# A decoder pipeline that runs on over the rounds, with the copy of the scores moved to the exponentials

## The chip, the cores and the metric

The kernel runs on one core of a Trainium2 chip. The metric is the device time of one execution in microseconds (us). The engines are TensorE (PE; its weight loads are PEld), VectorE (DVE), ScalarE (ACT), GpSimd (POOL) and the DMA queue of SyncE (SP). The profile is of one execution.

## What is computed

Two layers over 64 sequences of 128 tokens with 128 features, in float32: six stages, each written to memory and read by the next (a Mamba block, cross attention, an expert layer, a trajectory layer, a decoder layer, a quantised feed-forward layer). The change is in the fifth, the decoder layer. Cut to what matters:

```python
x_self  = _prob_sparse_self_attn(x, out_w, out_b)     # 16 heads, 128 keys, top-k of each row kept
x = _layernorm(x + x_self, ln1_g, ln1_b)
x_cross = _mha_cross(x, memory, in_w, in_b, out_w, out_b)   # 16 heads, 77 keys, plain softmax
x = _layernorm(x + x_cross, ln2_g, ln2_b)
h = jax.nn.gelu(x @ ffn_w1.T + ffn_b1, approximate=False)
x = _layernorm(x + h @ ffn_w2.T + ffn_b2, ln3_g, ln3_b)
```

The self attention has no projections of its own: queries, keys and values are the token features. The number kept by its top-k is ceil(log(129)) = 5.

## The kernel before

`decoder_stage` goes over the 64 sequences in 16 groups of four (GB = 4). Its rounds are software pipelined by group: in round i the self attention is of group i + 1, the cross attention of group i, and the feed-forward part of group i - 1. So there are 18 rounds, -1 to 16: five written out, and a loop (`nc.Fori`) over rounds 1 to 14, which are the full ones. Every round is a block: at its end all engines meet at a barrier and all semaphores are cleared.

A round has 16 steps. The class `Attend` works through units. A unit is half the heads (8) of one sequence, so a batch (one sequence) is two units. Units 0 to 7 are the self attention ("top-k units"), 8 to 15 the cross attention ("whole units"). A top-k unit passes through these pieces, each a method of `Attend`:

- `pool_keys` (L1120, POOL): the masked keys `de_a_km`, once for a batch.
- `pe_scores` (L1136): the scores into PSUM banks 0 and 1. There is only one such pair of banks for all units.
- `act_copy` (L1217): the scores from PSUM into `de_a_sp`, which frees the banks.
- `dve_largest` (L1280 to L1290): the eight largest of each row, the negative maximum `de_a_nb` (L1284), and the marking of those kept.
- `act_exp` (L1228): eight exponentials, one for each head, into `de_a_e`.
- `dve_pick` (L1297): all but the kept ones set to zero.
- `pe_turn` (L1152): eight transposes into banks 4 and 5.
- `act_turned` (L1240): these into `de_a_pt`.
- `pe_values` (L1163): times the values, into bank 6.

A whole unit has no copy and no top-k: `dve_shift` (L1308, L1312) reads the scores from PSUM in two halves, subtracts the maximum, and frees the banks; one exponential follows (L1233). After both units of a batch come `act_values` (L1247), `pe_back` (L1172, four transposes), `dve_normalise` (L1318, L1322), `pe_out` (L1177), `act_out` (L1253), `pe_project` (L1181) and `dve_add` (L2076 or L2083, with the statistics of the layer norm behind it).

No scheduler is at work: each engine's order is the order of the code. In step t an engine runs what `pe_step`, `act_step` and `dve_step` say:

- PE: `project` (odd steps), scores of unit t + 2, values of t - 1, turn of t; for whole units the scores come after the turn. Then `back` (odd) or `out` (even).
- ACT: `act_out` (odd), the copy of unit t + 1, the exponentials of t, `act_values` (odd), `act_turned` of t - 1.
- DVE: largest of t + 1, pick of t (or shift of t), then add (odd) or normalise (even).

Step 0 has the scores, copies and largest of units 0 and 1 as well, and step 15 the whole drain: the last turn, values and two chains of back, normalise, out, project and add. A unit never crosses the end of a round.

`decoder_stage` places the other work of the round at fixed steps, behind `Attend`'s part of the step: transposes, queries, keys and values of the cross attention (steps 0 to 3), the feed-forward part (layer norm of group i - 1 at steps 0 to 2, first matmul L2281 with its copies L2323 at 3 to 6, Gelu L2327 at ACT's step 6, second matmul L2287 at PE's step 6, its sum and statistics L2354 at DVE's step 7), and layer norms.

Of the kernel before, what the change touches and what calls it, by code (L numbers as in the profile page):

```python
# [1065 lines left out]
ATTEND_SEMS = ["km", "left", "score", "cp", "mx", "mr", "shift", "exp", "pick", "tr", "pt", "pv", "ot", "back", "rs", "o", "otp", "ots", "proj", "added"]  # L1066
# [6 lines left out]
class Attend:  # L1073

# [19 lines left out]
    def start(self, kinds, made=0):  # L1094
        self.kinds, self.made = kinds, made
        self.units = 2 * len(kinds)
        self.picked = 2 * sum(k.topk for k in kinds)

    def sem(self, name):
        return self.s[self.pre + "_" + name]  # L1100

# [14 lines left out]
    def pool_keys(self, pool, n, kind):  # L1116
        b, nk = n % GB, kind.nk
        if n >= 2:
            pool.wait_ge(self.sem("score"), 2 * (n - 1))
        self.nc.gpsimd.tensor_tensor(self.km[n % 2][:, :, 0:nk], kind.k(b).unsqueeze(1).to_broadcast([P, H, nk]),  # L1120
                                     self.hmask[:].unsqueeze(2).to_broadcast([P, H, nk]), ALU.mult).then_inc(self.sem("km"), 1)
# [3 lines left out]
    def pe_scores(self, pe, t):  # L1125
        n, half = divmod(t, 2)
        kind, b = self.kinds[n], n % GB
        if n + 1 > self.made:
            pe.wait_ge(self.sem("km"), n + 1 - self.made)
        if 1 <= t <= self.picked:  # L1130
            pe.wait_ge(self.sem("cp"), t)
        for j in range(2):
            if t > self.picked:
                pe.wait_ge(self.sem("shift"), 2 * (t - self.picked) - 1 + j)
# [11 lines left out]
    def pe_turn(self, pe, t):  # L1146
        nk = self.kinds[t // 2].nk
        pe.wait_ge(self.sem("pick" if t < self.picked else "exp"), t + 1)
        if t:
            pe.wait_ge(self.sem("pt"), t)  # L1150
# [4 lines left out]
    def pe_values(self, pe, t):  # L1155
        n, half = divmod(t, 2)
        kind, b = self.kinds[n], n % GB
        pe.wait_ge(self.sem("pt"), t + 1)
        if half == 0 and n >= 1:
            pe.wait_ge(self.sem("ot"), n)  # L1160
# [6 lines left out]
    def pe_back(self, pe, n):  # L1167
        pe.wait_ge(self.sem("ot"), n + 1)
        if n >= 1:
            pe.wait_ge(self.sem("added"), n)  # L1170
# [4 lines left out]
    def pe_out(self, pe, n):  # L1175
        pe.wait_ge(self.sem("o"), n + 1)
        self.nc.tensor.transpose(self.bank[:, 7, 0:P], self.o[:], self.ident[:]).then_inc(self.sem("otp"), 1)  # L1177

    def pe_project(self, pe, n):
        pe.wait_ge(self.sem("ots"), n + 1)  # L1180
        self.nc.tensor.matmul(self.bank[:, 7, P:P + D], self.ots[:], self.kinds[n].w_o, start=True, stop=True).then_inc(self.sem("proj"), 1)  # L1181

    def pe_step(self, pe, t):
        if t == 0:
            self.pe_scores(pe, 0)
            self.pe_scores(pe, 1)
        if t % 2 == 1 and t >= 5:
            self.pe_project(pe, (t - 5) // 2)
        if t + 2 <= self.picked and t + 2 < self.units:
            self.pe_scores(pe, t + 2)  # L1190
        if t:
            self.pe_values(pe, t - 1)
        self.pe_turn(pe, t)
# [4 lines left out]
        if t % 2 == 0 and t >= 4:  # L1198
            self.pe_out(pe, (t - 4) // 2)
        if t == self.units - 1:  # L1200
            last = self.units // 2 - 1
            self.pe_values(pe, t)
            for n in (last - 1, last):
                if n == last:
                    self.pe_back(pe, n)
                self.pe_out(pe, n)
                self.pe_project(pe, n)
# [3 lines left out]
    def act_copy(self, act, t):  # L1211
        nk = self.kinds[t // 2].nk
        act.wait_ge(self.sem("score"), t + 1)
        if t >= 2:
            act.wait_ge(self.sem("exp"), t - 1)
            act.wait_ge(self.sem("mr"), t - 1)
# [1434 lines left out]
```

## Time and profile before

| | us |
|---|---|
| median of 3 runs | 10324.21 (10296.58 to 10332.49) |
| the profiled execution | 10370.39 |
| its span | 10368.6 |
| decoder stage in it, from its first to its last instruction | about 2011 |
| full rounds, 14 of them | 121.1 each |

Over the span PE is busy 69% of the time, DVE 69%, ACT 41%, POOL 47%. These are averages over six stages with different limits. In the decoder stage the granted TensorE clock is 0.81 on average.

The profile is read like this. A timeline row gives start, duration, engine, line, operation, output <- input, the number of instructions merged in it, and in brackets the idle time ahead of it with what ended it. A windows row gives busy time and instruction count of each engine in a stretch, the granted clock (1.0 is 2.4 GHz, 0.5 is 1.2 GHz) and the DMA share. A waits row gives who waited for whom, the sum, the number of times, and the longest.

### The profile page before, as it was taken

What the parts mean: (1) busy time and instruction counts of PE and PEld (TensorE: products, weight loads), DVE (VectorE), ACT (ScalarE), POOL (GpSimd) and SP (SyncE); (2) the same over time, 40 slices, a digit from 0 to 9 for tenths busy, and PEclk for the clock granted to TensorE, in tenths of its full rate; (3) what the DMA queues carried; (4) which work ended last, traced back from release to release, by engine and by line L of the source; (5) the groups of instructions that cost most, each with busy time, mean ns of one, the idle gap of its engine ahead of it and who ended that gap; (6) DMA issues with size and microseconds to landing.
All of it is one profiled execution on the core that took longest, in us unless ns stands there. A gap on an engine that the chain in (4) does not pass through costs nothing. (4 is left out here: it accounts for less than half of the span.)

```text
span 10368.6 us, 93901 instructions
## 1 busy us (share of the span) xinstructions
PE 7195.5 (69%) x25835; PEld 3940.7 (38%) x25835; DVE 7140.9 (69%) x15339; ACT 4254.7 (41%) x8479; POOL 4829.1 (47%) x2704
## 2 busy tenths in 40 slices
PE   5888788878887888788877555555434777777723
PEld 2333333333333333355555333334222444444411
DVE  5999799979997999844343666666545655666456
ACT  3555455545554555511111122222113555555522
POOL 4888688868886888711111333333212323333300
PEclk8888888888888888866665777777556888888855
DMA  4333333333333333300000544444200000000000
GB/s 165 143 148 154 134 149 143 144 135 144 143 153 137 145 143 144 139 13 13 13 17 17 140 129 132 130 128 126 76 16 18 7 9 10 8 8 8 8 21 17
DMA packets 362092, 913.03 MB, mean 88 GB/s; under 512 B 27857, under 2 KB 254585, under 8 KB 293497
## 3 DMA queue, kind: packets, MB, share of 16 engines
q1 hardware_dynamic: 319033, 700.55, 17.8%
q0 software_dynamic: 42880, 210.80, 7.3%
q14 instruction: 153, 1.25, 0.0%
q8 instruction: 26, 0.43, 0.0%
HBM read 867.99 MB, written 56.70 MB: 89 GB/s over the span
## 5 line engine op out<-in xcount | busy, mean ns | idle before, releaser
L376 POOL TENSOR_TENSOR mb_dBu<-mb_dtu,mb_rows_b 128x1024 f32<-128x1024 f32 x1036 | 2423.8, 2357 | 322.0 <-POOLq L63 172.5
L390 DVE TENSOR_TENSOR_SCAN mb_bank<-mb_bank,mb_dBu 128x1024 f32<-128x1024 f32 x704 | 1612.5, 2290 | 90.1 <-PEq L63 90.1
L361 ACT ACTIVATE mb_bank<-mb_dt,mb_a_neg 128x508 f32<-128x508 f32 x2056 | 1314.6, 670 | 0.8
L430 PE MATMUL mb_bank<-mb_hcd,ident 128*128 128x512 f32 x2560 | 1265.1, 622 | 53.5 <-DVE mb_hcd L404 53.5
L430 PE MATMUL mb_bank<-mb_hcp,ident 128*128 128x512 f32 x1280 | 800.5, 759 | 351.6 <-POOL mb_hcp L413 351.6
L1643 POOL DMA_INDIRECT ex_rows<-in_ex_table,ex_idx x536 | 520.3, 971 | 959.5 <-PE ex_bank L1728 702.6
L413 POOL TENSOR_TENSOR mb_hcp<-mb_hs,mb_rows_c 128x1024 f32<-128x1024 f32 x320 | 752.0, 2350 | 368.3 <-DVE mb_hs L390 366.7
L404 DVE TENSOR_TENSOR mb_hcd<-mb_bank,mb_rows_c 128x1024 f32<-128x1024 f32 x704 | 862.1, 1225 | 31.4
L430 PEld LDWEIGHTS mb_bank<-mb_hcd,ident 128*128 128x128 f32 x2560 | 500.9, 202 | 769.9 <-issue 589.1
L390 DVE TENSOR_TENSOR_SCAN mb_hs<-mb_bank,mb_dBu 128x1024 f32<-128x1024 f32 x320 | 730.9, 2284 | 51.6 <-ACT mb_bank L361 51.6
L430 PEld LDWEIGHTS mb_bank<-mb_hcp,ident 128*128 128x128 f32 x1280 | 286.5, 237 | 805.8 <-POOL mb_hcp L413 476.8
L203 PE MATMUL mb_bank<-mb_h_ch,mb_w_conv 128*128 128x512 f32 x1088 | 517.4, 620 | 0.0
L1152 PE MATMUL de_bank<-ident,de_a_e 128*128 128x128 f32 (+1 forms) x2048 | 366.7, 337 | 196.4 <-DVE de_a_e L1297 196.4
L732 POOL TENSOR_TENSOR xa_n_rs<-xa_n_mv,minus_half 128x4 f32<-128x4 f32 x48 | 48.3, 1006 | 899.2 <-DVE xa_n_mv L721 899.2
L358 ACT ACTIVATE mb_bank<-mb_zeros 128x8 f32<-128x8 f32 x1028 | 174.4, 170 | 703.7 <-DVE mb_hcd L404 337.5
L1726 PE MATMUL ex_bank<-ex_w_out,ex_hidT 128*128 128x128 f32 x256 | 74.0, 442 | 541.2 <-issue 458.2
L1120 POOL TENSOR_TENSOR de_a_km<-de_xT,hmask 128x2048 f32<-128x2048 f32 x65 | 235.3, 3621 | 348.7 <-POOLq L63 324.3
L1152 PEld LDWEIGHTS de_bank<-ident,de_a_e 128*128 128x128 f32 (+1 forms) x2048 | 290.1, 177 | 269.5 <-DVE de_a_e L1297 228.0
L1615 PE MATMUL ex_bank<-ex_w_sim,ex_xT 128*128 128x512 f32 x544 | 315.2, 709 | 78.0 <-DVE ex_i L1626 51.6
L1136 PE MATMUL de_bank<-de_a_km,de_xT 128*128 128x512 f32 x512 | 295.8, 708 | 88.1 <-PEq L63 49.9
L861 PEld LDWEIGHTS xa_bank<-xa_vx,xa_a_pt 77*128 77x128 f32 x2048 | 338.3, 258 | 13.2 <-issue 2.6
L861 PE MATMUL xa_bank<-xa_vx,xa_a_pt 77*128 77x9 f32 x2048 | 340.3, 304 | 0.0
(358 smaller groups left out, 14436.7 us busy)
## 6 DMA issues: line engine op xcount, KB each, us to landing
mb_rows_b<-bc_rows SPq DMA_DIRECT2D x268, 1024.0 KB, 7.8
mb_rows_c<-bc_rows SPq DMA_DIRECT2D x264, 1024.0 KB, 6.8
mb_r_tok<-stream SPq DMA_DIRECT2D x76, 256.0 KB, 2.8
mb_r_post<-stream SPq DMA_DIRECT2D x68, 256.0 KB, 2.8
stream<-mb_r_post SPq DMA_DIRECT2D x68, 256.0 KB, 2.3
ex_rows<-in_ex_table,ex_idx POOLq DMA_INDIRECT x536
bc_rows<-mb_xp SPq DMA_DIRECT2D x68, 64.0 KB, 1.6
xa_r_tok<-stream SPq DMA_DIRECT2D x17, 256.0 KB
```

The lines of the kernel that those rows point to most:

```text
L203: m = nc.tensor.matmul(bank[:, M0 + c], w_conv[:, k, c * P:(c + 1) * P], h_ch[:, :, k:k + SEQ], start=(k == 0), stop=(k == DC - 1))
L361: e = nc.scalar.activation(da_of(n)[:, c * GB:(c + 1) * GB, 1:], dt[q][:, c].rearrange("p (b t) -> p b t", b=GB)[:, :, 1:], ACT.Exp, scale ...
L376: nc.gpsimd.tensor_tensor(by_c(dBu[m % RING][:]), by_c(chains(dtu[q][:])), over_c(rows_b[:, n]), ALU.mult).then_inc(s["mb_dbu"], 1)
L390: nc.vector.tensor_tensor_scan(flat(to), flat(da_of(n)), flat(dBu[n % RING][:]), 0.0, ALU.mult, ALU.add).then_inc(s["mb_scan"], 1)
L404: nc.vector.tensor_tensor(by_c(hcd[k % 3][:]), by_c(da_of(n)), over_c(rows_c[:, n]), ALU.mult).then_inc(s["mb_hcd"], 1)
L413: nc.gpsimd.tensor_tensor(by_c(hcp[k % 2][:]), by_c(hs[k % 2][:]), over_c(rows_c[:, n]), ALU.mult).then_inc(s["mb_hcp"], 1)
L430: m = nc.tensor.matmul(bank[:, B_Y + c], ident[:], part[:, c * GB:(c + 1) * GB], start=False, stop=False)
L861: m = nc.tensor.matmul(self.bank[:, 6, at:at + VW], self.pt[u % 2][:, h], vx(b, hf * HH + h), start=True, stop=True)
L1136: m = self.nc.tensor.matmul(self.scores_at(j, kind.nk), kind.q(b), self.km[n % 2][:, h0:h0 + 4, 0:kind.nk], start=True, stop=kind.bias is ...
L1152: m = self.nc.tensor.transpose(self.bank[0:nk, 4 + h // 4, (h % 4) * P:(h % 4 + 1) * P], self.e_of(t, nk)[:, h], self.ident[:])
L1615: nc.tensor.matmul(bank[:, j], xT[self.q][:, b], w_sim[:, 4 * j:4 * j + 4], start=True, stop=True).then_inc(p["sim"], 1)
L1643: nc.gpsimd.indirect_dma_start(rowsb[b][:, h], None, w["table"], bass.IndirectOffsetOnAxis(idx[b][:, h:h + 1], 0)).then_inc(got[b], 16)
```

## The change

Three things are changed together, all in the decoder stage.

First, the units run on over the rounds. `Attend.start` is now given the kinds of the round before, of this one and of the next, and a step may touch a unit below 0 (of the round before) or above 15 (of the next). Round i, at steps 14 and 15, makes the scores and the copies of the next round's units 0 and 1 and, on DVE, the largest of its unit 0; what was the drain of units 14 and 15 and of the last three batches lies in steps 0 to 5 of the next round. The barrier and the clearing of semaphores stay: `wait` and `upto` work out from tables of steps how many increments of this round have to be awaited. There is one more round, -2, at the start; seven rounds are written out and the loop runs over 1 to 13.

Second, the order in a step. ACT: the exponentials of t, the copy of t + 2 (it was t + 1, ahead of the exponentials), `act_out`, `act_values`, `act_turned` of t - 1. PE: scores of t + 2, values of t - 1, `project`, turn of t (`project` was ahead of all).

Third, the other work is moved to later steps, since batches of the last round end in steps 1 to 5: layer norm n2 from steps 0 and 1 to 3 and 4, its transposes from 2 to 5, the first feed-forward matmul from 3 to 5 to 6 and 7, the Gelu from ACT's step 6 to 8, the second matmul from PE's step 6 to 8, its sum from DVE's step 7 to 9, n3, n4 by one or two steps. POOL makes the keys at even steps, two batches ahead.

```diff
+UNIT_STEPS = {"left": -2, "score": -2, "cp": -2, "mx": -1, "mr": -1, "shift": 0, "exp": 0, "pick": 0, "tr": 0, "pt": 1, "pv": 1}
+BATCH_STEPS = {"km": -4, "ot": 3, "back": 3, "rs": 4, "o": 4, "otp": 4, "ots": 5, "proj": 5, "added": 5}
-    def start(self, kinds, made=0):
-        self.kinds, self.made = kinds, made
-        self.units = 2 * len(kinds)
-        self.picked = 2 * sum(k.topk for k in kinds)
+    def start(self, before, now, after):
+        self.per = len(now)
+        self.kinds = before + now + after
+    def upto(self, name, i):
+        total = 0
+        for j in range(-2 * self.per, i + 1):
+            step, kind = (j + UNIT_STEPS[name], self.unit(j)) if name in UNIT_STEPS else (2 * j + BATCH_STEPS[name], self.batch(j))
+            if step >= 0 and kind is not None and name not in (WHOLE_ONLY if kind.topk else TOPK_ONLY):
+                total += 2 if name == "shift" else 1
+        return total
...
     def pe_step(self, pe, t):
-        if t == 0:
-            self.pe_scores(pe, 0)
-            self.pe_scores(pe, 1)
-        if t % 2 == 1 and t >= 5:
-            self.pe_project(pe, (t - 5) // 2)
-        if t + 2 <= self.picked and t + 2 < self.units:
-            self.pe_scores(pe, t + 2)
-        if t:
-            self.pe_values(pe, t - 1)
-        self.pe_turn(pe, t)
-        if self.picked < t + 2 < self.units:
-            self.pe_scores(pe, t + 2)
+        there, early = self.unit(t + 2) is not None, not self.whole(t + 1)
+        if there and early:
+            self.pe_scores(pe, t + 2)
+        if self.unit(t - 1) is not None:
+            self.pe_values(pe, t - 1)
+        if t % 2 == 1 and self.unit(t - 5) is not None:
+            self.pe_project(pe, (t - 5) // 2)
+        if self.unit(t) is not None:
+            self.pe_turn(pe, t)
+        if there and not early:
+            self.pe_scores(pe, t + 2)
...
     def act_step(self, act, t):
-        if t == 0 and self.picked:
-            self.act_copy(act, 0)
-        if t % 2 == 1 and t >= 5:
+        if self.unit(t) is not None:
+            self.act_exp(act, t)
+        if self.topk(t + 2) and not self.whole(t + 1):
+            self.act_copy(act, t + 2)
+        if t % 2 == 1 and self.unit(t - 5) is not None:
             self.act_out(act, (t - 5) // 2)
-        if t + 1 < self.picked:
-            self.act_copy(act, t + 1)
-        self.act_exp(act, t)
-        if t % 2 == 1 and t >= 3:
+        if t % 2 == 1 and self.unit(t - 3) is not None:
             self.act_values(act, (t - 3) // 2)
-        if t:
+        if self.unit(t - 1) is not None:
             self.act_turned(act, t - 1)
-        if t == self.units - 1:
...
+        if self.topk(t + 2) and self.whole(t + 1):
+            self.act_copy(act, t + 2)
...
-                        if t == 6 and has_ffn:
+                        if t == 8 and has_ffn:
                             act.wait_ge(p["f1s"], FC)
                             nc.scalar.activation(hT[:], f1s[:], ACT.Gelu).then_inc(p["gelu"], 1)
...
-        round_of(-1, True, False, False)
-        round_of(0, True, True, False)
-        with nc.Fori(1, GROUPS - 1) as i:
-            round_of(i, True, True, True)
-        round_of(GROUPS - 1, False, True, True)
-        round_of(GROUPS, False, False, True)
+        for i in (-2, -1, 0):
+            round_of(i, i)
+        with nc.Fori(1, GROUPS - 2) as i:
+            round_of(i, 1)
+        for i in range(GROUPS - 2, GROUPS + 1):
+            round_of(i, i)
```

How the instructions stand now. ACT, steps 4 and 5 of a full round, before (`de_a_sp` is the copy of the scores, `de_a_e` the exponentials, `de_a_pt` the turned unit, `de_a_ot` and `de_a_ots` belong to the end of a batch):

```order
L1217 ACTIVATE de_a_sp<-de_bank 128x8x128
L1228 ACTIVATE de_a_e<-de_a_sp,de_a_nb 128x128 x8
L1240 ACTIVATE de_a_pt<-de_bank 128x1024
L2323 ACTIVATE de_f1s<-de_bank,de_vecs 128x512
L1253 ACTIVATE de_a_ots<-de_bank 128x128
L1217 ACTIVATE de_a_sp<-de_bank 128x8x128
L1228 ACTIVATE de_a_e<-de_a_sp,de_a_nb 128x128 x8
L1247 ACTIVATE de_a_ot<-de_bank 128x512
L1240 ACTIVATE de_a_pt<-de_bank 128x1024
```

The same two steps now:

```order
L1251 ACTIVATE de_a_e<-de_a_sp,de_a_nb 128x128 x8
L1242 ACTIVATE de_a_sp<-de_bank 128x8x128
L1262 ACTIVATE de_a_pt<-de_bank 128x1024
L1043 ACTIVATE de_xn<-de_a,de_n_shift,de_n_rstd 128x128 x4
L1251 ACTIVATE de_a_e<-de_a_sp,de_a_nb 128x128 x8
L1242 ACTIVATE de_a_sp<-de_bank 128x8x128
L1273 ACTIVATE de_a_ots<-de_bank 128x128
L1268 ACTIVATE de_a_ot<-de_bank 128x512
L1262 ACTIVATE de_a_pt<-de_bank 128x1024
```

The copy went from ahead of the exponentials to between them and the turned unit, and is now of the unit after next; the eviction for `de_a_pt` stands behind it, in odd steps behind `de_a_ots` and `de_a_ot` too.

PE, step 9 of a full round (whole units; `de_a_ots` is the operand of `project`, `de_a_pt` of the values, `de_a_e` of the turn, `de_a_km` of the scores), before:

```order
L1181 MATMUL de_bank<-de_ws,de_a_ots 128x128
L1163 MATMUL de_bank<-de_a_pt,de_vx 32x128 x8
L1152 MATMUL de_bank<-ident,de_a_e 77x128 x8
L1136 MATMUL de_bank<-de_a_km,de_qT 128x308 x2
L1172 MATMUL de_bank<-ident,de_a_ot 128x128 x4
```

Now, with the second feed-forward matmul of step 8 ahead of it:

```order
L2282 MATMUL de_bank<-de_w,de_hT 128x128 x16
L1199 MATMUL de_bank<-de_a_pt,de_vx 32x128 x8
L1216 MATMUL de_bank<-de_ws,de_a_ots 128x128
L1188 MATMUL de_bank<-ident,de_a_e 77x128 x8
L1173 MATMUL de_bank<-de_a_km,de_qT 128x308 x2
L1207 MATMUL de_bank<-ident,de_a_ot 128x128 x4
```

`project` (L1181, now L1216) went from ahead of the values to behind them.

## Rows read from the trace of the kernel before

**Rows 1.** Windows of core 0: stretch, busy of five engines, clock, DMA.
```profile
8077.60:9773.50 1695.90, 1228.50 (x8008) 808.21 (x8008) 1041.63 (x4396) 968.84 (x1974) 541.58 (x350) 0.82 0.03 8
...
8578.00:8630.00 52.00, 39.81 (x276) 26.96 (x274) 39.51 (x182) 38.49 (x81) 11.00 (x6) 0.89 0.01 3
```

**Rows 2.** Timeline, PE: a round's first scores, first turn, side transposes, next round.
```profile
8562.09 3.75 PE L1136 MATMUL de_bank<-de_a_km,de_xT 128*128 128x512 f32 x4 [2.11 <-PEq L63]
...
8577.17 1.97 PE L1152 MATMUL de_bank<-ident,de_a_e 128*128 128x128 f32 x8 [5.07 <-DVE de_a_e L1297]
8578.94 1.06 PE L2251 MATMUL de_bank<-ident,de_xn 128*128 128x128 f32 x4
...
8681.94 1.22 PE L1136 MATMUL de_bank<-de_a_km,de_xT 128*128 128x512 f32 x1 [2.11 <-PEq L63]
```

**Rows 3.** Timelines, DVE and POOL: a top-k step; the masked keys beside L1284.
```profile
8571.79 1.64 DVE L1280 MAX8 de_a_m<-de_a_sp 128x8 f32<-128x128 f32 x8
...
8577.03 1.64 DVE L1280 MAX8 de_a_m<-de_a_sp 128x8 f32<-128x128 f32 x8
...
8586.27 2.75 DVE L1284 TENSOR_SCALAR de_a_nb<-de_a_m 128x8 f32<-128x8 f32 x1
...
8585.38 3.61 POOL L1120 TENSOR_TENSOR de_a_km<-de_xT,hmask 128x2048 f32<-128x2048 f32 x1
```

**Rows 4.** Timelines, PE and ACT, steps 3 to 6: pieces of a top-k unit.
```profile
8601.03 1.88 PE L1136 MATMUL de_bank<-de_a_km,de_xT 128*128 128x512 f32 x4
8602.84 0.64 PE L1163 MATMUL de_bank<-de_a_pt,de_vself 128*32 128x128 f32 x16
8604.78 1.09 PE L1152 MATMUL de_bank<-ident,de_a_e 128*128 128x128 f32 x8 [1.30 <-DVE de_a_e L1297]
...
8606.20 1.02 ACT L1217 ACTIVATE de_a_sp<-de_bank 128x1024 f32<-128x1024 f32 x1
8607.10 2.44 ACT L1228 ACTIVATE de_a_e<-de_a_sp,de_a_nb 128x128 f32<-128x128 f32 x8
8609.44 0.58 ACT L1247 ACTIVATE de_a_ot<-de_bank 128x512 f32<-128x512 f32 x1
8609.91 1.01 ACT L1240 ACTIVATE de_a_pt<-de_bank 128x1024 f32<-128x1024 f32 x1
```

**Rows 5.** Timelines, ACT, PE and DVE: the Gelu and what waits for it.
```profile
8617.93 1.28 ACT L2327 ACT_TABLE_LOAD   x1
8619.22 1.91 ACT L2327 ACTIVATE de_hT<-de_f1s 128x2048 f32<-128x2048 f32 x1
...
8621.18 3.84 PE L2287 MATMUL de_bank<-de_w,de_hT 128*128 128x128 f32 x32 [0.80 <-ACT de_hT L2327]
...
8625.16 1.23 DVE L1297 SCALAR_TENSOR_TENSOR de_a_e<-de_a_mr,de_a_e 128x1024 f32<-128x1024 f32 x1 [5.47 <-ACT de_a_e L1228]
8627.15 0.69 DVE L2354 TENSOR_TENSOR de_a<-de_b_f,de_bank 128x512 f32<-128x512 f32 x1
```

**Rows 6.** Timeline, DVE: first halves of units 8, 9, 10 and 15; an addition.
```profile
8629.48 0.47 DVE L1308 TENSOR_REDUCE de_a_mx<-de_bank 128x4 f32<-128x308 f32 x1
...
8634.50 0.47 DVE L1308 TENSOR_REDUCE de_a_mx<-de_bank 128x4 f32<-128x308 f32 x1
...
8638.31 0.29 DVE L2076 TENSOR_TENSOR de_a<-de_b_own,de_bank 128x128 f32<-128x128 f32 x1 [1.84 <-PE de_bank L1181]
...
8639.15 0.45 DVE L1308 TENSOR_REDUCE de_a_mx<-de_bank 128x4 f32<-128x308 f32 x1
...
8666.66 0.47 DVE L1308 TENSOR_REDUCE de_a_mx<-de_bank 128x4 f32<-128x308 f32 x1
```

**Rows 7.** Waits of DVE over the stage: who waited for whom, us, times, longest.
```profile
DVE de_a_m L1280 <- ACT de_a_sp L1217: 114.1, 63, 12.4
```

**Rows 8.** Groups by line over the stage (16 rounds have these): busy us, mean ns.
```profile
L2281 PE MATMUL de_bank<-de_y2T,de_w 128*128 128x512 f32 x128 | 74.2, 692 | 1.7 <-ACT de_y2T L2318 1.7
...
L2264 PE MATMUL de_bank<-de_wv,de_cT 128*77 128x128 f32 x128 | 30.6, 420 | 0.6 <-ACT de_kT L2315 0.6
```

More of the change, by code:

```diff
@@ L1092, in __init__, with batch, unit, topk @@
             self.nb = sb(pre + "_nb", [P, 2, HH])
-    def start(self, kinds, made=0):
-        self.kinds, self.made = kinds, made
-        self.units = 2 * len(kinds)
-        self.picked = 2 * sum(k.topk for k in kinds)
+    def start(self, before, now, after):
+        self.per = len(now)
+        self.kinds = before + now + after
+    def batch(self, n):
+        i = n + self.per
+        return self.kinds[i] if 0 <= i < len(self.kinds) else None
+    def unit(self, t):
+        return self.batch(t // 2)
+    def topk(self, t):
+        return self.unit(t) is not None and self.unit(t).topk
+    def whole(self, t):
+        return self.unit(t) is not None and not self.unit(t).topk
     def sem(self, name):
         return self.s[self.pre + "_" + name]
+    def upto(self, name, i):
[5 more added lines that the diff above has]
+        return total
+    def wait(self, engine, name, i, less=0):
+        n = self.upto(name, i) - less
+        if n > 0:
+            engine.wait_ge(self.sem(name), n)
     def e_of(self, t, nk):
@@ L1126, in pe_scores @@
         n, half = divmod(t, 2)
[L1127 to L1131, printed above, removed]
+        kind, b = self.batch(n), n % GB
+        self.wait(pe, "km", n)
+        if not self.whole(t - 1):
+            self.wait(pe, "cp", t - 1)
         for j in range(2):
-            if t > self.picked:
-                pe.wait_ge(self.sem("shift"), 2 * (t - self.picked) - 1 + j)
+            if not self.topk(t - 1):
+                self.wait(pe, "shift", t - 1, less=1 - j)
             h0 = half * HH + 4 * j
@@ L1156, in pe_values @@
         n, half = divmod(t, 2)
[L1157 to L1160, printed above, removed]
+        kind, b = self.batch(n), n % GB
+        self.wait(pe, "pt", t)
+        if half == 0:
+            self.wait(pe, "ot", n - 1)
         for h in range(HH):
@@ L1286, in dve_largest @@
         dve.drain()
-        if t >= 2:
-            dve.wait_ge(self.sem("pick"), t - 1)
+        self.wait(dve, "pick", t - 2)
         for h in range(HH):
@@ L2159, in _, with kinds_of, round_of @@
                 pool.wait_ge(p["xts"], 1)
-                at.pool_keys(pool, 0, own)
         s0.clear()
         s.clear()
-        def round_of(i, has_own, has_cross, has_ffn):
-            kinds = [own] * (GB if has_own else 0) + [cross] * (GB if has_cross else 0)
-            at.start(kinds, made=1 if has_own else 0)
-            first, end = (0 if has_own else 8), (16 if has_cross else 8)
-            base = 4 if not has_own else 0
+        def kinds_of(i):
+            return [own if 0 <= i + 1 < GROUPS else None] * GB + [cross if 0 <= i < GROUPS else None] * GB
+        def round_of(i, shape):
+            at.start(kinds_of(shape - 1), kinds_of(shape), kinds_of(shape + 1))
+            has_own, has_cross, has_ffn = (0 <= shape + k < GROUPS for k in (1, 0, -1))
+            has_next = 0 < shape + 2 < GROUPS
             with nc.Block() as block:
@@ L2242, in there @@
                             pe.wait_ge(p["qs"], 1)
                             pe.wait_ge(p["vb"], 1)
-                    for t in range(16):
-                        there(t)
-                        if first <= t < end:
-                            at.pe_step(pe, t - first)
+                        at.pe_step(pe, t)
                         if t == 0 and has_cross:
```

246 lines of the change are left out of this document (106 added, 140 removed).

## The prediction, as it was put on record

> **What bounds the kernel now.** The change is confined to the decoder stage, so I first took the windows of that stage: the 14 full rounds take 1695.9 us, 121.1 each, at a granted clock of 0.82 [rows 1]; outside them are about 315 of the stage's 2011 us. Nothing else of the kernel can move, so the sum is over one round, times 14, and the edges. Then I followed one round in the timelines of PE, ACT, DVE and POOL; it runs from 8562.1 to 8681.9 (119.8) [rows 2]. I cut it in four:
>
> 1. Start to first turn, 8577.2: 15.1 us, plus the 0.2 by which POOL starts ahead, 15.3. Scores, copies and largest of units 0 and 1 in sequence; PE has idled 5.07 before the turn [rows 2].
> 2. First turn to the first subtraction, 8629.5: 52.3 us [rows 6]. DVE is busy 39.5 of 52.0, PE 39.8 [rows 1]: near DVE's pace, not at it. A top-k step costs DVE 5.24 (8571.79 to 8577.03) [rows 3]. It waits 114.1 us in the stage for copies [rows 7], some 7 a round, and once a round 5.47 for the exponentials behind the Gelu [rows 5].
> 3. First to last subtraction, 8666.7: 37.2 us [rows 6], the whole units. No engine is full; a chain of hand-overs sets it.
> 4. Last subtraction to the next round: 15.3 us [rows 2, 6], the drain, with about 1.1 of barrier in it.
>
> So 30 of 120 us are filling and draining, and the question is what of them comes back inside the steps.
>
> **Part by part.** I give the time of each stretch after the change by adding the rows' durations along whatever is last; instructions on one engine overlap by 0.1, hand-overs cost 0.05.
>
> *Stretch 1.* Unit 0's largest and both copies are already there. DVE starts the largest of unit 1 at once. But POOL starts batch 2's masked keys at once too, 3.6 us, and the small L1284 ends only when they end: beside such an instruction it took 2.75, from 8586.27 to 8589.02, where the keys ended at 8588.99 [rows 3]. So 3.7, then the marking 2.4, then the pick 1.2: the first turn starts at 7.4. Gain 7.9.
>
> *Stretch 2.* Taken out: the 5.47 wait and the 2.3 of L2354 and its statistics (8627.15 to 8629.48) [rows 5, 6]. DVE never again waits for a copy. But a new ring closes. PE's order is scores(t+2), values(t-1), turn(t); ACT's is exponentials, copy(t+2), turned(t-1). The eviction for turned(t-1) was ready to go, and now is queued behind the copy, which waits for scores that PE runs only after turn(t-1). One step of the ring: scores 1.9, copy 0.95, eviction 1.05, values 0.6, turn 1.0 [rows 4] with hand-overs 5.6; an odd step has the ACT pieces of `act_out` and `act_values` in it (0.7), project (0.3) and back (0.5), an even one out (0.1). A pair is 12.5, 6.2 a step. There is a second ring of the same size: project, which now comes after values, then DVE's add 0.84, largest and marking 4.1, pick 1.2, turn, scores, copy, the two small pieces, eviction, values, project: 12.8 a pair. DVE alone would need 6.0 (5.24 and, a pair, 0.84 and 0.6). Seven steps at 6.3: 44. In the ring lie also PE's side matmuls, since the scores come behind them: the transposes of step 0, 1.5 [rows 2]; queries and keys 1.6 (two passes of 512 columns are half of the scores' 1.88 [rows 4], the keys' less); values' 1.9 (30.6 by 16) and half of 4.6 (74.2 by 16) [rows 8]; n2's transposes 0.55, half a turn. Together 7.8. Once more the port-bound L1284 meets keys at step 4: 1.7. That makes 53.5 at the full clock. The turn takes 1.97 at 1.2 GHz against 1.09 at 2.4 [rows 2, 4]; the granted clock of this stretch is 0.89 [rows 1], and PE now stops twice in each step (for eviction and pick). Of the 20 or so us of PE work not already counted slow, I add 12%: 2.5. So 56.0 against 52.3: **loss 3.7**.
>
> *Stretch 3.* The Gelu is now here. From unit 8's subtraction: until unit 9's scores are done 2.8, back 0.5, two first matmuls 2.0, eviction 0.7, table load 1.28, Gelu 1.9, second matmul 3.85 [rows 5], values and project 1.0, add 0.85, L2354 with statistics 2.3: unit 10's subtraction starts 17.2 later. Before it was 9.7 [rows 6]: 7.5 more. For the other pairs: before, project runs while ACT is still at the exponential, so the add comes 3.8 after unit 9's subtraction and unit 10's starts at 4.65 [rows 6]. With project behind values, the add also waits for exponential, eviction and values: 6.7 to 7.0. In return the even step is shorter (4.0), because PE is through with its turn when the scores' banks come free. A pair is 10.8, as before; n4's statistics fall between. I take 1.0 for all of it, within -1 and +3. **Loss 8.5**.
>
> *Stretch 4.* The drain goes, but from the last subtraction there follow scores 16, copy, scores 17, copy, the two small pieces, eviction, values, project, turn, back: 1.95 + 1.4 + 1.05 + 1.9 + 1.1 + 0.7 + 0.95 + 0.65 + 0.3 + 1.1 + 0.55 + 1.15 barrier = 12.8 at the full clock, 14.2 with the slow one, against 15.3. Gain 1.1. DVE's largest of unit 16 (4.1) is hidden behind this chain.
>
> Sum for a round: -7.9 + 3.7 + 8.5 - 1.1 = +3.2. Fourteen: +45. *Edges.* The new round -2 costs a fill and a barrier, some 15, less the 3.6 of keys that leave the set-up: +11. Rounds -1 and 0 have the gains and no Gelu: -8. In round 15 the feed-forward part waits for the drain of round 14 before unit 8's scores may start, and round 16 gets a drain of 12 that round 15 loses: +5. Together +8. Total +53, on the profiled execution 10370.4 to 10423, and on the median 10324.2 to 10377. I say **10375**.
>
> What I cost at nothing: POOL's keys, since four of eight are now made two batches ahead, under the cover of PE's ring (if the wait for `added` delays them, round by round 1 to 2 us); SP's loads, issued as before; the code of two more written-out rounds.
>
> A rule against my sum: PE idles 5.07 in one piece ahead of the first turn [rows 2], and such idle time is what is removed. The Trainium skill, Perfetto Trace Analysis, section Optimization Strategies, says that where the matmul engine idles for other engines, those that block the critical path should be optimized to keep it going. By that the round would get the fill and the drain back and lose nothing: the first rival.
>
> **The rivals.** *The fill is saved and the rings don't bind* (faster, 0.25). This holds if the eviction finds its turn and its engine free before DVE's pick of the next unit is done. For it: DVE is busy 39.5 of 52.0 [rows 1], so it is close to the bound before, and copies two steps ahead take its 7 us of waits away. Against it: the ring's rows add to more than DVE's 6.0 even at the full clock. Its price: stretch 2 at 7 steps of 6.0 and 1.7 is 43.7, a gain of 8.6; with stretch 3's 8.0 lost, 7.9 and 1.1 gained: -9.6 a round, -134, about 10190. It decides when a step's ring is under 6.0 us; half way there (side matmuls hidden behind evictions) it is -45 to -60, 10270.
>
> *They cancel* (0.25): the ring binds, but the clock is no worse than the rows at 2.4 GHz and the add finds project done: -0.5 to +1 a round, 10300 to 10350. This is also what a pipeline would give in which the border costs as much as a full step.
>
> *The clock falls* (0.05): PE, stopped twice in each step, is granted 1.2 GHz for most of stretches 2 and 3. Scores then take 3.75 [rows 2] and a turn 1.97: some 12 us a round more, 10500.
>
> **How the numbers follow.** The forecast, rings and moved Gelu eat more than the fill gives, has 0.45, and 10350 to 10420 for its own range. A measurement of this kernel can tell about 0.3%, 31 us, from no change. Slower by more: 0.45 and 0.05, less a little of the forecast's low end, 0.48. Within: 0.24. Faster: 0.28. Cases of both signs are open, so the range goes from the halfway case of the first rival with some more, 10225, to 10460, which leaves out the full rival at 10190 and the fallen clock.
>
> **What would show it.** After the change: the first turn 7 to 8 us after a round's start; DVE's waits for copies gone, and instead DVE waiting for PE's project before L2076 and L2083, 3 to 5 us at steps 1 and 3; ACT's L1217 waiting for scores, with L1240 right behind it; PE idle ahead of the values, for the eviction, about 2 us a step; the subtractions of units 8 and 10 some 17 us apart; full rounds of 124 us. Wrong would be: own steps at 6.0 with DVE without a gap (first rival), or a Gelu that is hidden behind the whole units' chain, which would take 7.5 us a round off my sum.

## The result and the profile after

| | us |
|---|---|
| before, median of 4 runs | 10310.4 (10295.88 to 10332.49) |
| after, median of 4 runs | 10427.81 (10420.67 to 10434.9) |
| ratio | 1.0108, 95% interval 1.0094 to 1.0121 |
| predicted | 10375, from 10225 to 10460 |

The change makes the kernel 1.1% slower, by some 111 to 117 us, about twice the 53 that were forecast. The span of the profiled execution is 10424.7. The two profiled spans are just 56.1 apart, since the one before (10368.6) was a long execution of its kernel: the stages ahead of the decoder, which are not changed, took 50 us more in it (VectorE's first instruction of the decoder is at 7870.73, and at 7820.47 after). The decoder stages themselves are 104 us apart. Windows of the changed kernel, with the columns of [rows 1]: the 13 rounds of the loop, then in one round the second and the third stretch of the prediction:

```profile
8028.46:9694.90 1666.44, 1142.02 (x7436) 760.46 (x7436) 936.27 (x4082) 897.16 (x1834) 509.19 (x325) 0.81 0.03 8
8549.60:8605.50 55.90, 39.39 (x252) 26.64 (x252) 39.31 (x187) 33.71 (x79) 15.99 (x10) 0.82 0.01 3
8605.50:8656.20 50.70, 36.62 (x254) 25.49 (x255) 20.61 (x69) 22.83 (x34) 17.08 (x14) 0.80 0.00 0
```

A round takes 1666.44 / 13 = 128.2 us, where it took 121.1 [rows 1]. PE is busy 87.8 us a round in both kernels (1142.02 / 13, and 1228.50 / 14 of [rows 1]). Nothing was added to its work; it stands idle 7 us longer. All 14 full rounds, round 14 among them, take 1787 against 1696, +91; the edges make up the rest of the 104.

Three rounds of each kernel, divided as in the prediction (us, mean of three rounds):

| | before | after | change | predicted |
|---|---|---|---|---|
| 1, start to first turn | 15.1 | 8.0 | -7.1 | -7.9 |
| 2, to unit 8's subtraction | 52.3 | 55.2 | +2.9 | +3.7 |
| 3, to unit 15's subtraction | 37.5 | 50.8 | +13.3 | +8.5 |
| 4, to the next round | 15.9 | 14.4 | -1.5 | -1.1 |
| sum | 120.7 | 128.4 | +7.7 | +3.2 |

The rounds of one profile are not all alike. Over 13 rounds of each kernel the changes are -7.2, +3.3, +12.8 and -1.8, together +7.1; where three rounds would mislead below, the mean of 13 is given and called so.

The start of a round, timelines of DVE and PE; the round starts at 8541.5:

```profile
8544.18 1.64 DVE L1295 MAX8 de_a_m<-de_a_sp 128x8 f32<-128x128 f32 x8 [5.45 <-issue]
...
8549.58 0.69 PE L1188 MATMUL de_bank<-ident,de_a_e 128*128 128x128 f32 x2 [1.64 <-DVE de_a_e L1310]
```

The first turn is 8.1 us after the round's start and PE has idled 1.64 ahead of it, where it idled 5.07 [rows 2]. The fill is gone.

Step 3 of the same round, timelines of ACT, PE and DVE, beside [rows 4]:

```profile
8571.08 1.02 ACT L1242 ACTIVATE de_a_sp<-de_bank 128x1024 f32<-128x1024 f32 x1 [2.84 <-PE de_bank L1173]
8572.00 0.27 ACT L1273 ACTIVATE de_a_ots<-de_bank 128x128 f32<-128x128 f32 x1
8572.16 0.60 ACT L1268 ACTIVATE de_a_ot<-de_bank 128x512 f32<-128x512 f32 x1
8572.63 1.04 ACT L1262 ACTIVATE de_a_pt<-de_bank 128x1024 f32<-128x1024 f32 x1
...
8573.73 1.08 PE L1199 MATMUL de_bank<-de_a_pt,de_vself 128*32 128x128 f32 x16 [2.69 <-ACT de_a_pt L1262]
8574.74 0.80 PE L1216 MATMUL de_bank<-de_wo,de_a_ots 128*128 128x128 f32 x2
8575.33 1.72 PE L1188 MATMUL de_bank<-ident,de_a_e 128*128 128x128 f32 x8
...
8575.58 0.29 DVE L2085 TENSOR_TENSOR de_a<-de_b_c,de_bank 128x128 f32<-128x128 f32 x1 [5.02 <-PE de_bank L1216]
```

It reads from top to bottom as one chain. ACT stands 2.84 us before the copy, for the scores; the eviction is fourth in its queue; PE stands 2.69 before the values, for the eviction; project and turn come behind; and DVE, with its pick done (it ended at 8570.56), stands 5.02 for the project. This is what the prediction described. ACT waits with work in its queue whose operands are ready.

The Gelu in the same round, ACT, PE and DVE, beside [rows 5]:

```profile
8611.15 1.28 ACT L2321 ACT_TABLE_LOAD   x1
8612.45 1.91 ACT L2321 ACTIVATE de_hT<-de_f1s 128x2048 f32<-128x2048 f32 x1
8614.37 1.28 ACT L1256 ACT_TABLE_LOAD   x1
8615.67 0.72 ACT L1256 ACTIVATE de_a_e<-de_a_e 128x616 f32<-128x616 f32 x1
...
8614.41 3.84 PE L2282 MATMUL de_bank<-de_w,de_hT 128*128 128x128 f32 x32 [1.25 <-ACT de_hT L2321]
8618.18 0.64 PE L1199 MATMUL de_bank<-de_a_pt,de_vx 77*32 77x128 f32 x16
8618.75 0.49 PE L1216 MATMUL de_bank<-de_ws,de_a_ots 128*128 128x128 f32 x2
...
8605.48 0.45 DVE L1318 TENSOR_REDUCE de_a_mx<-de_bank 128x4 f32<-128x308 f32 x1
...
8619.28 0.29 DVE L2078 TENSOR_TENSOR de_a<-de_b_own,de_bank 128x128 f32<-128x128 f32 x1 [8.02 <-PE de_bank L1216]
...
8620.12 0.69 DVE L2350 TENSOR_TENSOR de_a<-de_b_f,de_bank 128x512 f32<-128x512 f32 x1
...
8622.45 0.47 DVE L1318 TENSOR_REDUCE de_a_mx<-de_bank 128x4 f32<-128x308 f32 x1
```

Units 8 and 10 are 8622.45 - 8605.48 = 17.0 us apart; the prediction had 17.2.

The rest of stretch 3. POOL, ACT and DVE at the places where something besides the chain holds it up:

```profile
8625.93 2.27 POOL L1158 TENSOR_TENSOR de_a_km<-de_kT,hmask 128x1232 f32<-128x1232 f32 x1 [15.34 <-PE de_bank L1173]
8628.15 1.02 POOL L1035 TENSOR_TENSOR de_n_rstd<-de_n_mv,minus_half 128x4 f32<-128x4 f32 x1
...
8639.78 3.61 POOL L1158 TENSOR_TENSOR de_a_km<-de_xT,hmask 128x2048 f32<-128x2048 f32 x1 [5.96 <-PE de_bank L1173]
...
8629.49 1.65 ACT L1043 ACTIVATE de_xn<-de_a,de_n_shift,de_n_rstd 128x128 f32<-128x128 f32 x4 [3.41 <-POOL de_n_shift L1037]
...
8634.92 0.29 DVE L2078 TENSOR_TENSOR de_a<-de_b_own,de_bank 128x128 f32<-128x128 f32 x1 [5.65 <-PE de_bank L1216]
...
8642.84 0.57 DVE L1029 TENSOR_SCALAR de_n_mv<-de_n_mv 128x4 f32<-128x4 f32 x1
```

POOL's part of n3 (L1035) had its input at 8622.5 but stands behind keys that wait for the scores of unit 11; ACT waits 3.41 for it, with exponential 11 behind. The addition at step 11 waits 5.65 for the project; in the kernel before it waits 1.84 there, as much as at step 9 in [rows 6]. And the little L1029 of n4 takes 0.57 (0.17 where no keys are beside it): it ends at 8643.41, with the keys (8643.39).

### The profile page after: what moved, and what is told of

Read it like the earlier page. It is cut to its first block and busy times, and to the rows that moved or that the text cites. A ratio compares the mean times of both kernels' runs of the same rounds, so it can differ in the third digit from the quotient of the medians.

```text
span 10424.7 us, 93915 instructions
## 1 busy us (share of the span) xinstructions
PE 7189.1 (69%) x25815; PEld 3945.7 (38%) x25831; DVE 7114.2 (68%) x15339; ACT 4252.2 (41%) x8478; POOL 4836.1 (46%) x2701
## 5 line engine op out<-in xcount | busy, mean ns | idle before, releaser
L1158 POOL TENSOR_TENSOR de_a_km<-de_kT,hmask 128x1232 f32<-128x1232 f32 x64 | 149.6, 2338 | 523.5 <-PE de_bank L1173 523.5
L1251 ACT ACTIVATE de_a_e<-de_a_sp,de_a_nb 128x128 f32<-128x128 f32 x1024 | 312.9, 402 | 73.5 <-PEq L63 73.2
```

The costliest lines, as they stand in the source:

```text
L1251: m = self.nc.scalar.activation(self.e_of(t, nk)[:, h], self.sp[t % 2][:, h, 0:nk], ACT.Exp, scale=kind.scale, bias=self.nb[:, t % 2, h:h ...
```

## The experiments

Each runs beside the kernel before on the same chip; ratios are against that kernel. Rounds are the mean of the 13 from the first full one, from the loads at their starts, unless other is said. In the expectations the kernels are also called by number: the first is "copy last", the second "project early", the third both, the fourth "second matmul later".

**Copy last.** ACT's copy goes to the end of the step, behind the eviction, as in the kernel before, where it opened the next step.

```diff
     def act_step(self, act, t):
             self.act_exp(act, t)
-        if self.topk(t + 2) and not self.whole(t + 1):
-            self.act_copy(act, t + 2)
...
             self.act_turned(act, t - 1)
-        if self.topk(t + 2) and self.whole(t + 1):
+        if self.topk(t + 2):
             self.act_copy(act, t + 2)
```

> The changed kernel (10428) with one thing undone: ScalarE's copy of unit t+2 stands at the end of the step, behind the eviction of the turned unit t-1. Ring theory (the eviction is queued behind a copy that waits for scores, which PE runs only after the turn): own steps fall from about 8 us to DVE's pace, first turn to unit 8's subtraction from 55.9 to 48-52 us, the waits of the copy for scores no longer hold the values, so 4 to 8 us a round, 10320 to 10370. Rival (side matmuls, clock and the project behind the values set the own steps, not the copy): 55 us stay, 10410 to 10430.

Measured: 10281.24, ratio 0.9952 (0.9935 to 0.9968); a round 119.0 us, 9.2 less than after. The second stretch falls from 55.2 to 47.8, the drain from 14.4 to 12.7, the third stays at 50.8. Waits over the decoder stage, of after and then of this kernel (who waited for whom: us, times, longest):

```profile
ACT de_a_sp L1242 <- PE de_bank L1173: 336.1, 94, 7.1
PE de_bank L1199 <- ACT de_a_pt L1262: 327.5, 139, 3.6
```

```profile
PE de_bank L1199 <- ACT de_a_pt L1262: 130.4, 85, 3.6
...
ACT de_a_sp L1242 <- PE de_bank L1173: 116.5, 74, 4.1
```

Two thirds of ACT's waits for scores go, and with them 200 us of PE's for the eviction. The ring theory holds, and with more than I gave it: the time is under the forecast of 10320.

**Project early.**

```diff
     def pe_step(self, pe, t):
-        if self.unit(t - 1) is not None:
-            self.pe_values(pe, t - 1)
         if t % 2 == 1 and self.unit(t - 5) is not None:
             self.pe_project(pe, (t - 5) // 2)
+        if self.unit(t - 1) is not None:
+            self.pe_values(pe, t - 1)
```

> The changed kernel with PE's project ahead of the values in an odd step (behind the scores in the top-k steps). If the project behind the values makes the whole units' odd steps 7 to 8.8 us long, unit 8's to unit 15's subtraction goes from 50.7 to 45-47 us: 4 to 5 us a round, about 10365. Rival (a pair of whole units keeps its length, the even step grows as the odd one shrinks, as the prediction had it): stays at 50, 10415 to 10430. The own steps hardly change by either, since the eviction is what is late there.

Measured: 10288.73, ratio 0.9967 (0.9953 to 0.9981), well under the 10365 expected; a round 118.8. The third stretch falls from 50.8 to 46.6, as expected, but the second falls as much, from 55.2 to 51.0, which I had ruled out. Step 1 of a round, ACT, PE and DVE:

```profile
8614.91 0.27 ACT L1273 ACTIVATE de_a_ots<-de_bank 128x128 f32<-128x128 f32 x1
...
8615.54 1.04 ACT L1262 ACTIVATE de_a_pt<-de_bank 128x1024 f32<-128x1024 f32 x1
...
8615.23 0.49 PE L1216 MATMUL de_bank<-de_wo,de_a_ots 128*128 128x128 f32 x2 [1.28 <-ACT de_a_ots L1273]
8616.64 0.64 PE L1199 MATMUL de_bank<-de_a_pt,de_vself 128*32 128x128 f32 x16 [0.92 <-ACT de_a_pt L1262]
...
8615.76 0.29 DVE L2085 TENSOR_TENSOR de_a<-de_b_c,de_bank 128x128 f32<-128x128 f32 x1 [1.92 <-PE de_bank L1216]
```

The eviction still stands behind the copy, but PE runs the project in the gap before it, so that DVE's next largest starts some 1.4 us earlier (the addition waits 1.92, in after 3.33 at this step). So the second ring of the prediction, through the addition, was on the path among the top-k units too; and of the whole units' pairs, "I take 1.0 for all of it" was too little.

**Both.**

> Both of the two edits above. If the copy's place and the project's place are two independent costs: the sum, 8 to 13 us a round, 10250 to 10320, at or below the kernel before. If they are the same cost seen twice: no better than the better one of the two, about 10350.

Measured: 10182.71, ratio 0.9862 (0.9846 to 0.9879), under both forecasts. The stretches are 7.9, 47.6, 46.2 and 11.2 (mean of 13 rounds); a round takes 112.9. That is 15.3 less than after, of the 9.2 and 9.4 of the two alone. In the second stretch copy last alone already returns all of it (47.7, mean of 13): with the eviction no longer late, a project behind it isn't late either, as I read it. In the third stretch copy last returns nothing (50.8, and 50.4 after) and project early everything (46.2 alone and 46.2 with both). In the drain both count: 14.3 after, 12.7 and 13.4 with one, 11.2 with both. This kernel is 1.4% faster than the one before.

**Second matmul later.** The second feed-forward matmul, its sum, n3 and n4 a step later each; on PE and DVE:

```diff
-                        if t == 8 and has_ffn:
+                        if t == 9 and has_ffn:
                             pe.wait_ge(p["gelu"], 1)
...
-                        if t == 9 and has_ffn:
+                        if t == 10 and has_ffn:
                             dve.wait_ge(p["f2"], 1)
```

> The changed kernel with the second feed-forward matmul at PE's step 9 instead of 8, and what hangs on it (its sum, n3, the sum with b_3, n4) one step later each. Theory (PE and DVE stand still for Gelu and the matmul, 17.0 us from unit 8's to unit 10's subtraction): that gap goes to 11-13 us, 4 to 6 us a round, about 10360. Rival (the chain sum, n3, n4 then ends last and the round's end waits for the store): the gap shrinks, the end of the round grows from 14.0 us by as much, 10420 to 10440.

Measured: 10454.26, ratio 1.0127 (1.011 to 1.0144); a round 129.7. My theory fell. The rival's time was just missed, and its cause is there in small part: the drain is 15.0 against 14.3 (mean of 13), because it is 15.9 to 17.0 in four rounds; in the three rounds compared it is 14.4, as after. There units 9 and 10 are 11.3 apart instead of 13.2, but units 10 and 11 are 10.2 instead of 4.9. DVE at those two units:

```profile
8630.93 0.29 DVE L2078 TENSOR_TENSOR de_a<-de_b_own,de_bank 128x128 f32<-128x128 f32 x1 [8.40 <-PE de_bank L1216]
...
8631.77 0.45 DVE L1318 TENSOR_REDUCE de_a_mx<-de_bank 128x4 f32<-128x308 f32 x1
...
8639.92 0.69 DVE L2350 TENSOR_TENSOR de_a<-de_b_f,de_bank 128x512 f32<-128x512 f32 x1 [3.06 <-PE de_bank L2282]
...
8642.25 0.47 DVE L1318 TENSOR_REDUCE de_a_mx<-de_bank 128x4 f32<-128x308 f32 x1
```

The addition waits 8.40 even without the matmul, because ACT is held by Gelu and table loads; and a step later the matmul holds up unit 11 in its turn. Taking a block off one wait does not hide it if it is queued ahead of the next.

**Gelu left out.**

```diff
-                            nc.scalar.activation(hT[:], f1s[:], ACT.Gelu).then_inc(p["gelu"], 1)
+                            nc.scalar.activation(hT[:], f1s[:], ACT.Identity).then_inc(p["gelu"], 1)
```

> The changed kernel (10428) with ACT.Identity in place of the decoder's Gelu: the Gelu itself is left out, the pass over 128x2048 stays, and with it go the table load ahead of it and the one ahead of exponential 9, 1.28 us each. If the block Gelu, table loads, second matmul, exponential 9 stands wholly on the path: 2.56 us in each of 15 rounds with a feed-forward part and an exponential after it, -38, about 10390. Rival (another chain is as late at unit 10's subtraction): less than half of that, 10410 to 10430.

Measured: 10416.94, ratio 1.0087 (1.007 to 1.0104), against 1.0108. The intervals overlap, so the gain is small and its size uncertain: 11 us between the medians, 22 between the ratios, 0.9 us a round (127.3 against 128.2, mean of 13). Of the round's parts the gap between units 9 and 10 shows it, 11.9 instead of 13.2 in every full round. ACT and PE there:

```profile
8612.99 1.91 ACT L2321 ACTIVATE de_hT<-de_f1s 128x2048 f32<-128x2048 f32 x1
8614.81 0.71 ACT L1256 ACTIVATE de_a_e<-de_a_e 128x616 f32<-128x616 f32 x1
...
8614.96 3.84 PE L2282 MATMUL de_bank<-de_w,de_hT 128*128 128x128 f32 x32
```

The rival's range holds it, and so does its idea that another chain is as late: of the two loads just the first is on the path. The one ahead of exponential 9 (8614.37 in after) lies beside the second matmul's 3.84, which ends last.

**The kernel before, with the Gelu late.** The sum, n3 and n4 follow in the same way:

```diff
-                        if t == 6 and has_ffn:
+                        if t == 8 and has_ffn:
                             pe.wait_ge(p["gelu"], 1)
...
-                        if t == 6 and has_ffn:
+                        if t == 8 and has_ffn:
                             act.wait_ge(p["f1s"], FC)
                             nc.scalar.activation(hT[:], f1s[:], ACT.Gelu).then_inc(p["gelu"], 1)
```

> The kernel before (10327) with the third part of the change alone, as far as the feed-forward part goes: Gelu and second matmul at step 8 instead of 6, the sum with statistics at DVE's step 9 instead of 7, n3 and n4 as late as in the changed kernel. The prediction prices this at +7.5 us a round among the whole units and -7.8 among the top-k units (5.47 of wait and 2.3 of sum): within 0.3% of before, 10300 to 10350. Rival (a Gelu among the whole units costs more than one among the top-k units, since DVE has nothing of its own there): 3 to 5 us a round slower, 10370 to 10400.

Measured: 10347.04, ratio 1.0032 (1.002 to 1.0045); a round 123.0. The range I gave held it, but it is a loss, and its parts are not as priced: the second stretch gains 4.4 (52.3 to 47.9), not 7.8, since unit 7's pick still waits 3.44 us for exponentials:

```profile
8697.71 1.22 DVE L1297 SCALAR_TENSOR_TENSOR de_a_e<-de_a_mr,de_a_e 128x1024 f32<-128x1024 f32 x1 [3.44 <-ACT de_a_e L1228]
```

The third loses 6.7 (37.5 to 44.2). Net 2 us a round for moving the Gelu.

**Out first.** The third kernel with `act_out` ahead of the exponentials and `project` ahead of the scores.

```diff
     def act_step(self, act, t):
+        if t % 2 == 1 and self.unit(t - 5) is not None:
+            self.act_out(act, (t - 5) // 2)
         if self.unit(t) is not None:
             self.act_exp(act, t)
-        if t % 2 == 1 and self.unit(t - 5) is not None:
-            self.act_out(act, (t - 5) // 2)
```

> The third kernel with act_out first in ScalarE's odd step and project first in PE's, as both were in the kernel before. The addition then never waits for the exponentials: with the Gelu's two table loads and exponential 9 ahead of act_out it waited 7.25 us at step 9, 4.0 at step 11, 4.1 at step 7. Theory (the addition's wait is on the path in the odd steps of the whole units): 1.5 to 3 us at step 9 and 0.7 to 1 at three others, 3 to 5 us a round, 10115 to 10145. Rival (DVE then waits for scores instead, since PE's turn and scores come no earlier): 10170 to 10185.

Measured: 10228.47, ratio 0.9914 (0.9898 to 0.9931): half a per cent slower than without it. A round takes 114.9, 2.0 to 3.0 more than in the third kernel's two profiles; 1.2 of that is in the drain. ACT at step 13:

```profile
8580.10 0.28 ACT L1273 ACTIVATE de_a_ots<-de_bank 128x128 f32<-128x128 f32 x1 [8.57 <-PE de_bank L1212]
8580.28 0.72 ACT L1256 ACTIVATE de_a_e<-de_a_e 128x616 f32<-128x616 f32 x1
```

The same pattern as the copy's, made by me: a small instruction that waits for PE stands ahead of an exponential whose input was complete about 2 us earlier (8578.25). Two orders were changed at once here, and no run shows that this wait alone carries the loss.

With the second matmul later on top of it:

> The kernel with out and project first, and the second feed-forward matmul with all behind it one step later, as in the fourth. There the stall only moved, because the addition at step 9 waited 8.40 us behind Gelu, table loads, exponential and values. If the addition is what carried the stall: units 8 to 10 now 12 us apart instead of 16 or more, and 2 to 4 us a round better than without the later matmul, 10070 to 10110. Rival (exponential 9 and the eviction behind the table loads carry it, by turn and scores): as without it, within 15 us.

Measured: 10232.78, ratio 0.9918 (0.9901 to 0.9934), no different. Units 9 and 10 are now 6.6 apart, units 10 and 11 12.8 to 13.9, in the place of 12.4 and 4. The addition did carry the stall at unit 10; at unit 11 it is back.

**POOL's n3 ahead of the keys**, on the third kernel:

```diff
+                        if t == 10 and has_ffn:
+                            n3.pool(pool)
                         at.pool_step(pool, t)
...
-                        if t == 10 and has_ffn:
-                            n3.pool(pool)
```

> The third kernel (copy last and project early, 10183) with POOL's part of layer norm n3 ahead of the masked keys in step 10. In the profile of that kernel ScalarE waits 2.82 us for POOL's n3, which stands behind keys that wait for scores, and exponential 11 is queued behind it. If POOL's order there is on the path: the gap between the subtractions of units 11 and 12 (6.8 to 7.1) shrinks by about 2 us, 28 us in all, 10155. Rival (the n3 chain is late by itself and the keys are then late instead): no change, 10175 to 10190.

Measured: 10150.61, ratio 0.9843 (0.9823 to 0.9863). Since that overlaps with the third kernel's interval, the two ran once more side by side.

> The third kernel again (copy last, project early), beside the next on the same chip, because 10183 and 10151 were measured on different days of the chip and their intervals overlap. As before: 0.986 of the kernel before.

> The same with POOL's n3 ahead of the keys in step 10. In the profiles its rounds are 2.5 us shorter (110.3 against 112.8, of three rounds each), of which 1.3 between the first and last subtraction. If that is the order's doing: 20 to 35 us under the kernel beside it. If it is the way in which the rounds of one profile differ from each other: within 10 us of it.

Measured: 10189.15, ratio 0.987 (0.9854 to 0.9885), and 10149.71, ratio 0.9826 (0.9812 to 0.9841). The intervals are apart: 39 us for two lines in POOL's order, and 1.7% under the kernel before, the best version here. In the means of 13 rounds the gain is where the edit is: the gap between units 11 and 12 goes from 7.0 (in both profiles of the third kernel) to 5.4 (in both of this one), the one behind it from 7.6 and 7.2 to 6.6. The third stretch goes from 46.2 and 45.7 to 43.6 and 43.7, the second by less than 1.

**Gelu at ACT's step 7**, on the kernel with n3 first; `y2T` goes from 6 to 5 as well:

```diff
-                        if t in (7, 8) and has_ffn:
-                            for c in (2 * t - 14, 2 * t - 13):
+                        if t in (6, 7) and has_ffn:
+                            for c in (2 * t - 12, 2 * t - 11):
                                 act.wait_ge(p["f1"], c + 1)
...
-                        if t == 8 and has_ffn:
+                        if t == 7 and has_ffn:
                             act.wait_ge(p["f1s"], FC)
```

> The kernel with copy last, project early and n3 first (10151), with ScalarE's feed-forward work one step earlier: y2T at step 5, f1s at 6 and 7, Gelu at ScalarE's step 7, PE's second matmul left at step 8. If what costs is that Gelu, table load and second matmul follow each other with PE and DVE empty (units 9 to 10 12.4 us apart): PE now finds the Gelu done, that gap falls to about 8 and unit 8's to 9's grows by less than 2, 2 to 4 us a round, 10095 to 10120. Rival (the first matmuls of step 6 are now waited for by ScalarE ahead of the exponentials 7 and 8, and the top-k steps grow): 10140 to 10170.

Measured: 10380.47, ratio 1.0046 (1.003 to 1.0063): 2% slower than without it, and far outside both ranges. ACT behind step 7:

```profile
8586.59 0.69 ACT L2315 ACTIVATE de_f1s<-de_bank,de_vecs 128x512 f32<-128x512 f32 x1 [6.57 <-PE de_bank L2274]
...
8592.67 0.72 ACT L1256 ACTIVATE de_a_e<-de_a_e 128x616 f32<-128x616 f32 x1
8593.30 1.00 ACT L1262 ACTIVATE de_a_pt<-de_bank 128x1024 f32<-128x1024 f32 x1
8594.20 0.72 ACT L1256 ACTIVATE de_a_e<-de_a_e 128x616 f32<-128x616 f32 x1
```

ACT stands 6.57 us for the last two first matmuls, which PE runs at the end of step 7, behind turn and scores; the exponentials of units 8 and 9 are both queued behind. The rival had named this wait, ahead of exponentials 7 and 8, and priced it at under 20 us in all: the second stretch grows from 47.3 to 52.8, the third from 43.7 to 53.7 (mean of 13), and units 9 and 10 are 20.1 apart.

## Why the prediction was right, and where it was not

The direction and the mechanisms hold; the size was half of what was measured. The time lies in the stated range, but 8 us above the 10350 to 10420 that I gave the forecast itself.

- **Stretch 1**: -7.9 predicted, -7.1 measured. DVE's first instruction comes 2.7 us after PE's (8544.18 and 8541.50), with no releaser in the trace; that start was not in the sum. The kernel before has it too (8564.72 and 8562.09), but there the scores ran beside it.
- **Stretch 2**: +3.7 and +2.9, near by luck, since two errors cancel. The credit for the departed Gelu was 7.8; alone it is 4.4. So the rings, with what else was moved to this stretch, cost 55.2 - 47.9 = 7.3, not 11.5. Copy last returns 7.4 of it. The rings, then, were real and over-priced. Of their terms the clock's (2.5) looks near, as far as two rounds tell: in the round that starts at 8670.47 this stretch is granted 0.87 and takes 53.96, beside the 55.90 at 0.82 shown above. Which of the others was too large (the side matmuls with 7.8, or what a step costs) the runs don't separate. The pair of the first ring is also added up wrongly: its terms give 12.8, not 12.5; the 6.3 a step that was used fits the 12.8.
- **Stretch 3**: the step that failed, +8.5 against +13.3. The Gelu's pair came out: 7.5 predicted, 17.0 - 9.6 = 7.4 measured. Of that 0.8 is the project's place, which was in the chain (16.2 with project early); the Gelu moved alone gives 15.4. "I take 1.0 for all of it, within -1 and +3" was mis-sized: the other five gaps are 33.8 us instead of 27.9, +5.9. The runs account for all of it. In means of 13 rounds: 33.4 after and 28.0 before; with project early 30.0, with copy last too 30.0 and 29.4 (its two profiles), with POOL's n3 first 27.4 in both of its profiles. Two steps of the prediction failed there. I let the even step pay back what the odd one loses by the late project, and it does not; and I costed POOL's new order at nothing, under "the cover of PE's ring", while n3 waited in it behind keys that wait for PE. The L1029 beside the keys is in the third kernel and the one with n3 first too (0.58 to 0.99) and was not tried by itself.
- **Stretch 4**: -1.1 and -1.5.
- **Edges**: +8 predicted. The stage takes about 2115 us where it took 2011, and 91 of the 104 are in the full rounds: +13. No run takes the edges apart.
- The signs named under "what would show it" are there: first turn at 8.1, waits for the project 3.3 and 5.0 at steps 1 and 3, values waiting 2.0 to 2.7 for the eviction, 17.0 from unit 8 to 10; rounds of 128, not 124.
- **The rivals.** That the rings don't bind is refuted: the second stretch is 55.2 with them and 47.8 without. But the same idea is worth as much as its price said once the rings are cut: both edits and n3 first give 10150, where the rival said 10190. The fallen clock is in part there: the second stretch is granted 0.82, before 0.89 [rows 1]; it was no 170 us. No run changes the clock by itself.

The steps can be added up. Before 121.1 us a round; Gelu late, +1.9 (123.0); running on over the rounds, with copy and project kept from standing in the way and all else that was moved for it, -10.1 (112.9), of which the start gives 7.2, the drain 4.4 and the second stretch 0.4, and the third takes 1.9; copy ahead of the eviction and project behind the values, +15.3 (128.2). Running on was a good idea, and the order in a step spent it and more.

On the rule: PE's idle piece ahead of the first turn, 5.07 [rows 2], is 1.64 now, and PE idles 40.4 us a round instead of 33.3 (the rounds above less 87.8). The Trainium skill, Perfetto Trace Analysis, section Optimization Strategies, would have those engines optimized that block the critical path. Read as in the prediction, that such a gap is there for the taking, it is contradicted by the changed kernel, which put gaps of 2.0 to 2.7 into its top-k steps for it (327.5 us of PE waiting for evictions over the stage, 150.7 before), and borne out by the third kernel, where those waits are 61.9 (112.9 a round).

## What to carry to other kernels

Where each engine runs its queue in order, an instruction that waits for another engine must not stand ahead of one whose operands are ready; ask of each instruction moved forward what is queued behind it, and follow the answer once round the engines, since this fault was made four times here (copy, project, out first, Gelu at step 7; for out first its price is not shown) with the same look each time: an engine with an idle stretch that names a releaser, and ready work behind. When a pair of steps has a loss in one and a gain in the other, don't let them cancel unless a row shows the wait that absorbs it. And software pipelining over a border pays back part of the fill and the drain (here 11.6 of some 31 us, 10.1 net) only while no step gets longer, so write the order of a step first and then remove the border.

## What the hardware showed besides

The same kernel has rounds of two lengths. Two rounds next to each other of the third kernel (second measurement), windows of their first 55 us, with the columns of [rows 1]:

```profile
8464.00:8519.00 55.00, 35.67 (x245) 23.86 (x246) 47.47 (x210) 39.70 (x96) 20.02 (x11) 0.85 0.04 13
...
8577.10:8632.10 55.00, 36.05 (x274) 24.05 (x274) 48.26 (x217) 40.49 (x97) 20.30 (x11) 0.94 0.04 13
```

The granted clock is 0.85 in the one and 0.94 in the other; the rounds take 113.1 and 109.2 us, and 3.9 of it lies in the second stretch (49.3 and 45.4). The instructions are the same. The kernel before does it too: its rounds alternate between 119.8 us at 0.84 and 122.5 at 0.81, and the prediction followed one of the short kind; with project early they go from 115.3 at 0.90 to 123.3 at 0.81. In these the length goes with the granted clock, if not strictly (the third kernel also has rounds of 112.2 at 0.91); as no run holds the clock fixed, which of the two causes the other is not shown. Half of a per cent of a kernel like this can thus be which rounds are of the short kind, and three rounds from one profile can't rank two kernels 0.4% apart: those of this pair (110.5 and 110.3) look alike, where the timed runs are 39 us apart. The means of 13 rounds, 111.9 and 110.0, do tell them apart.
